# A message-passing kernel whose source columns come from copies and whose source rows come from gathers: 8 instead of 12 units of a round use column copies, and GpSimd gathers five more tiles

## The reference, cut to what matters

```
h_nodes = silu(x @ node_W1 + b) @ node_W2 + b                # 12500 x 64
h_edges = silu(edge_attr @ edge_W1 + b) @ edge_W2 + b        # 400000 x 64
msgs    = silu([h_nodes[dst], h_nodes[src], h_edges] @ msg_W1 + b) @ msg_W2 + b
agg     = segment_sum(msgs, dst) / max(counts, 1)
out     = layernorm(x + silu([x, agg] @ upd_W1 + b) @ upd_W2 + b) * ln_g + ln_b
result  = layernorm(x + out)
```

## Time and profile before

| | |
|---|---|
| median of 3 runs | 4963.27 us (4941.1 to 4977.42) |
| profiled execution: span from first to last instruction | 3612.0 us |
| profiled execution: its own time | not recorded for this kernel; the median is 1351.3 us above the span |
| TensorE (PE) busy | 2874.1 us, 80% |
| VectorE (DVE) busy | 2737.3 us, 76% |
| ScalarE (ACT) busy | 2994.3 us, 83% |
| GpSimd (POOL) busy | 2674.4 us, 74% |
| instructions in the trace | 103943 |
| DMA | 350.77 MB, mean 97 GB/s |

### The profile page before, as it was taken

How to read it: one execution, slowest core, us unless ns; L and a number is a source line. 1 busy time by engine, 2 the same in 40 slices (tenths; PEclk the granted TensorE clock), 3 DMA queues, 4 the chain that set the end, 5 groups by cost and what they waited for, 6 DMA issues and landing times.

```text
span 3612.0 us, 103943 instructions
## 1 busy us (share of the span) xinstructions
PE 2874.1 (80%) x16224; PEld 2219.4 (61%) x16224; DVE 2737.3 (76%) x20847; ACT 2994.3 (83%) x23073; POOL 2674.4 (74%) x2823
## 2 busy tenths in 40 slices
PE   4878888877878878888778888777778878877885
PEld 2666666666666666666666666656665656656664
DVE  4777778778777777777787777787777777877876
ACT  4998888888887888988888888888878888888785
POOL 4777777777777777777777777777777777777773
PEclk7687777677777777777777777777777776677766
DMA  7454444454444454444454444444444444444441
GB/s 225 78 113 100 87 94 100 89 102 96 95 95 86 96 102 90 101 100 88 93 103 85 102 96 95 99 95 87 98 92 99 101 89 96 90 92 102 96 95 43
DMA packets 263059, 350.77 MB, mean 97 GB/s; under 512 B 111714, under 2 KB 199121, under 8 KB 252514
## 3 DMA queue, kind: packets, MB, share of 16 engines
q1 hardware_dynamic: 169792, 246.77, 32.0%
q0 software_dynamic: 90624, 95.15, 14.5%
q10 hardware_dynamic: 1954, 2.14, 0.2%
HBM read 330.78 MB, written 13.01 MB: 95 GB/s over the span
## 4 chain that ended last, share of the span: by engine, by line
POOL 62%; issue 21%; PE 8%; DMA 4%; DVE 4%; DVEq 0%; ACT 0%; SPq 0%; ACTq 0%; POOLq 0%
POOL b_ring L834 62%; DMA b_ring<-b_table,src 4%; PE p_pre L696 2%; PE p_pre L702 1%; DVE colbuf L642 1%; PE p_sum L716 1%; PE p_hid L849 1%; DVE comb L939 1%; DMA work<-in_xT 1%; PE p_pre L705 0%; PE p_last L995 0%; PE p_last L996 0%; DVEq L627 0%; DVE stats L1032 0%; ACT colbuf L642 0%
## 5 line engine op out<-in xcount | busy, mean ns | idle before, releaser
L834 POOL DMA_INDIRECT b_ring<-b_table,src x2800 | 2652.0, 947 | 858.9 <-issue 844.8
L642 ACT COPY colbuf<-shared 64x4 uint8 x21134 | 2127.4, 190 | 159.9 <-issue 148.4
L642 DVE COPY colbuf<-shared 64x4 uint8 x17511 | 1377.6, 194 | 308.6 <-issue 301.9
L696 PE MATMUL p_pre<-wa_ring,comb 128*128 128x64 f32 x6250 | 1047.1, 329 | 0.0
L696 PEld LDWEIGHTS p_pre<-wa_ring,comb 128*128 128x128 f32 x6250 | 996.8, 245 | 0.9 <-issue 0.8
L727 ACT ACTIVATE comb<-p_hid,b_e 64x320 f32<-64x320 f32 x1250 | 652.8, 522 | 360.4 <-PE p_hid L849 350.9
L939 DVE SCALAR_TENSOR_TENSOR comb<-shared,p_const 64x640 f32<-64x640 int32 x625 | 554.0, 887 | 458.8 <-PE p_pre L696 336.2
L716 PEld LDWEIGHTS p_sum<-hot_ring,msg 128*65 128x65 f32 x6250 | 589.2, 181 | 500.0 <-DVE agg L949 265.0
L716 PE MATMUL p_sum<-hot_ring,msg 128*65 128x64 f32 x6250 | 649.5, 269 | 291.1 <-DVE agg L949 166.6
L702 PE MATMUL p_pre<-b_ring,ident 128*128 128x320 f32 (+1 forms) x1250 | 583.4, 559 | 341.4 <-DMA b_ring<-b_table,src 340.8
L849 PE MATMUL p_hid<-e_ring,w_e 128*128 128x320 f32 x1250 | 626.2, 591 | 49.0 <-DMA e_ring<-in_edgeT 40.0
(11 more groups left out here) (106 smaller groups left out, 599.2 us busy)
## 6 DMA issues: line engine op xcount, KB each, us to landing
e_ring<-in_edgeT SPq DMA_DIRECT2D x250, 320.0 KB
shared<-in_dst_row SPq DMA_DIRECT2D x125, 640.0 KB
b_ring<-b_table SPq DMA_DIRECT2D x3200, 0.2 KB
b_ring<-b_table,src POOLq DMA_INDIRECT x2800
e_ring<-in_edgeT SPq DMA_DIRECT2D x50, 400.0 KB
shared<-in_dst_row SPq DMA_DIRECT2D x25, 800.0 KB
wa_ring<-a_table SPq DMA_DIRECT2D x625, 16.0 KB
work<-in_xT SPq DMA_DIRECT2D x25, 250.0 KB
```

Of the source, the lines that this page charges most:

```text
L642: end = copy(colbuf[:, special % COLBUF, at:at + 1].bitcast(U8), of[j])
L696: return eng.matmul(p_pre[:, i % 2, k * H:(k + 1) * H], comb[:, i % COMBS, k * P:(k + 1) * P], wa_ring[:, i % RING, :], start=k == 0, stop ...
L834: eng.indirect_dma_start(b_ring[:, b_slot(i), k, :], None, b_table, bass.IndirectOffsetOnAxis(ap=src[:, u * TILES + k:u * TILES + k + 1], ...
```

## The change

The list of special units goes from 12 to 8, with smaller lists of columns. `ROW_TILE`, `load_rows`, `fetch_rows`, their semaphores and TensorE's wait for them are taken out, and GpSimd gathers the tiles: `by_pool(i)` becomes `gathered(i)`.

```
-SPECIAL = [1, 3, 5, 7, 9, 11, 13, 15, 17, 19, 21, 23]
+SPECIAL = [1, 4, 7, 10, 13, 16, 19, 22]
 COLS = dict(vector=58, scalar=70)
...
-LOAD = dict(vector=32, scalar=40)
-LISTED = 656
-ROW_TILE = (24, 3)
-ROWS_A_STEP = 8
-ROWS_FROM = 7
+LOAD = dict(vector=20, scalar=24)
+LISTED = 672
...
-    row_list_in = sem("row_list_in")
-    row_in = [sem(f"rows{q}_in") for q in range(4)]
...
     def gathered(i):
 
         return [k for k in range(TILES) if not (i in SPECIAL and k == TILES - 1)]
 
-    def by_pool(i):
-
-        return [k for k in gathered(i) if (i, k) != ROW_TILE]
...
-        load_rows(eng, 0)
-
-    def load_rows(eng, r):
...
-    def fetch_rows(eng, r, i):
...
-        for q, node in enumerate(nodes):
-            eng.dma_start(b_ring[first + q:first + q + 1, b_slot(unit), tile, :], b_table[ds(node, 1), :])\
-               .then_inc(row_in[q % len(row_in)], 16)
...
-        eng.wait_ge(row_list_in, 16 * ROUNDS + 16)
...
-            if 0 <= i - ROWS_FROM < P // ROWS_A_STEP:
-                fetch_rows(eng, r, i)
...
-            for k in by_pool(i):
+            for k in gathered(i):
                 eng.indirect_dma_start(b_ring[:, b_slot(i), k, :], None, b_table,
...
-            if j == ROW_TILE[0]:
-                for arrived in row_in:
-                    wait_alone(eng, arrived, (rr + 1) * (16 * P // len(row_in)))
```

More of the change, by code:

```diff
@@ L150, in program @@
         at += words
-    row_list = to_ab[0:1, :, :, :, :].rearrange("o s t q n -> o (s t q n)").bitcast(I32)[:, at:at + P]
-    assert at + P <= SR * 2 * 2 * GJ * H
+    assert at <= SR * 2 * 2 * GJ * H
     pad = sb("pad", [W, H], F32)
@@ L599, in gathered @@
         return [k for k in range(TILES) if not (i in SPECIAL and k == TILES - 1)]
-    def by_pool(i):
-        return [k for k in gathered(i) if (i, k) != ROW_TILE]
     def b_value(r, i):
-        each = [16 * len(by_pool(j)) for j in range(ROUND) if b_slot(j) == b_slot(i)]
-        so_far = [16 * len(by_pool(j)) for j in range(i + 1) if b_slot(j) == b_slot(i)]
+        each = [16 * len(gathered(j)) for j in range(ROUND) if b_slot(j) == b_slot(i)]
+        so_far = [16 * len(gathered(j)) for j in range(i + 1) if b_slot(j) == b_slot(i)]
         return sum(each) * r + sum(so_far)
@@ L745, in sync_first @@
         load_list(eng, LEADIN, LEADIN, HALF_AT, list_in[0])
-        load_rows(eng, 0)
-    def load_rows(eng, r):
-        eng.dma_start(row_list, a["rows"][ds(r * P, P)].unsqueeze(0)).then_inc(row_list_in, 16)
-    def fetch_rows(eng, r, i):
[L755 to L761, removed]
-        for q, node in enumerate(nodes):
-            eng.dma_start(b_ring[first + q:first + q + 1, b_slot(unit), tile, :], b_table[ds(node, 1), :])\
-               .then_inc(row_in[q % len(row_in)], 16)
-        if first + ROWS_A_STEP == P:
-            load_rows(eng, r + 1)
     def sync_last(eng):
-        eng.wait_ge(row_list_in, 16 * ROUNDS + 16)
         eng.wait_ge(list_in[0], 32 * ROUNDS + 32)
@@ L1091, in pool_general @@
         for u in range(EARLY):
-            eng.wait_ge(b_in[b_slot(u)], 16 * len(by_pool(u)))
+            eng.wait_ge(b_in[b_slot(u)], 16 * len(gathered(u)))
         with eng.Fori(0, UNITS) as u:
@@ L1208, in _laid_out @@
     d["dst_row"] = g["dst"].reshape(-1)
-    rows = g["src"].reshape(-1, ROUND, TILES, P)[:, ROW_TILE[0], ROW_TILE[1], :]
-    d["rows"] = np.concatenate([rows, np.zeros_like(rows[0:1])]).reshape(-1)
     special = g["src"].reshape(-1, ROUND, TILES, P)[:, SPECIAL, TILES - 1, :]
```

## The result

The changed kernel takes 4627.99 us, the median of four runs (4618.87 to 4634.18). The kernel before took 4960.24 us beside it, also of four (4941.1 to 4977.42). The ratio is 0.9333, 95% interval 0.9298 to 0.9368: 6.7% faster. I had forecast 3.2% slower and had given "faster by over 1%" one chance in ten.

What follows compares the result with a forecast made beforehand. GpSimd's gathers were taken to bound the kernel: a 3612.0 us span plus 156.5 us for 125 more gathers, with 1351.3 us around it held constant, gave 5120 us, 3.2% slower. The range was 5065 to 5200 us.

Steps and rivals of the forecast that it cites:

- 1351.3 us: Median time less profiled span, taken as time around the span and carried in the sum as a constant.
- What bounds the kernel: GpSimd's gathers bound it at 1.2519 us each, never held up by a full ring of source rows.
- Gathers: GpSimd's gathers go from 2800 to 2925, +125 at 1.2519 us each: +156.5 us, all on the bound.
- Pace of a gather: No change in GpSimd's pace as copies and single-row transfers go; at most 9 us either way.
- Column copies: 12,882 fewer copies, relieving ScalarE of 709 us and VectorE of 459 us, worth nothing while gathers bound.
- TensorE: Some 40 us less matmul work from fewer special tiles, off the path.
- SyncE: 3200 single-row DMAs go, relieving its queue of 1250 us; costed at nothing.
- B: Timed runs stretched evenly against the profile: a gather costs 1.720 us, 125 cost 215 us, 5178 us; chance 0.13.
- A: The forecast itself: gathers bound, the time around the span constant, 5120 us; chance 0.67.
- C: Time around the span shrinks with the program's instructions, by 292 us: 4828 us, faster; chance 0.10.
- D: Another engine or a transfer bounds the timed runs and hides the gathers: 4963 us, within 1%; chance 0.07.
- E: TensorE's clock falls to 1.2 GHz throughout with longer waits for gathers: 5426 us; chance 0.03.

Runs made afterwards that it cites:

- experiment 1: The kernel before, unchanged, profiled once more: 4977.24 us, with a span of 4974.7 us.
- experiment 15: The kernel after, with one of a unit's five sum matmuls done, four fifths of the sums left out: 4661.45 us, 0.9402 of the kernel before.
- experiments 2: The kernel before, still 12 special units, but without SyncE's single rows; GpSimd gathers that tile: 4688.55 us, 0.944 of the kernel before.
- 5: The kernel before with 8 special units; SyncE fetches 128 fixed rows, without node-number loads or register instructions: 4570.86 us, 0.9352 of the kernel before.
- 6: The kernel before, still 12 special units; SyncE fetches 128 fixed rows, without node-number loads or register instructions: 4641.0 us, 0.9356 of the kernel before.
- experiment 4: The kernel before with 8 special units; SyncE fetches 64 single rows instead of 128: 4557.64 us, 0.9328 of the kernel before.
- 8: The kernel before with 8 special units, single rows kept; ScalarE starts the edge feature and destination loads: 4987.71 us, 1.0072 of the kernel before.
- 9: The kernel after, with the edge feature and destination loads started by ScalarE instead of SyncE: 4877.25 us, 0.984 of the kernel before.
- 7: The kernel after, with 9600 unread semaphore increments on SyncE where the single rows stood: 4765.1 us, 0.9741 of the kernel before.
- 12: The kernel after, with 9600 semaphore increments on GpSimd ahead of the gathers in steps 7 to 22: 4767.39 us, 0.9637 of the kernel before.
- experiment 16: The kernel after, with each gather fetching 64 instead of 128 rows: 4608.57 us, 0.9301 of the kernel before.

## Why the prediction was wrong

**The step that failed first.** "I take the median as its time, so 1351.3 us is what lies around the span, and the sum carries it as a constant". No such time exists: in the repeated profile of the kernel before, span and time differ by 2.5 us (4974.7 and 4977.24), in the kernel after by 1.9. The trace was of an execution whose span is 26% shorter than the shortest timed one (4882.3 us). I had cited the Trainium skill (Runtime: NRT & Kernel Launch, The launch sequence), whose 9 to 15 us around a kernel say that 1351.3 us can't lie there, and set it aside as not explaining the gap. The traces agree that little lies around the span; the measured 1.9 and 2.5 us are below even that figure. That page of the Trainium skill spoke against the step, not only beside it.

**What bounds the kernel.** "So GpSimd is never held up by a full ring of source rows" holds for the execution that the earlier trace rows come from, and not for the timed ones, where it is held up for 1520 us (experiment 1).

**Gathers.** The count is right, x2925. But the +156.5 us, "all on the bound", is wrong: in the timed runs GpSimd has waits to put them into. 200 more of them together with 25,800 fewer copies (12 to 4 special units) leave the time within 1%; alone they were not tried.

**Pace of a gather.** Right: 953 ns median and about 1.25 us from one to the next when nothing is waited for (745.8 us of "issue" in 2433 gaps is 0.307 us each). The Trainium skill (SBUF — State Buffer, Who interferes with whom) has a VectorE copy in a two-port mode lock GpSimd out. No run here shows whether these copies run in such a mode. No lock shows in the gathers' durations, as in the earlier trace rows: one lasts 946 ns beside 17,511 copies, 952 beside 11,674, 948 beside none.

**Column copies.** "Worth nothing" was nearly right for the kernel after (1.1%, together with 100 more gathers, hardly told from none) and wrong by sign where the rows stay (+6.0%). No rival had such an interaction.

**TensorE.** That 40 us less of its work count for nothing fits: without four fifths of its sum matmuls the kernel was no faster, though at a lower clock (experiment 15).

**SyncE.** "TensorE's waits are for b_ring, not these, in the rows shown, so I cost the relief at nothing." This is the term that carries the result: the change gains 6.7%, and taking out the rows alone gains 5.6% of 4951.68 us, **277 us**, 263 in medians (4951.68 - 4688.55). I had the right queue and the right things behind it. The 1250 us for what it was relieved of were too low: with the 400 loads of node numbers, which I left out, the rows took 1680 us of SyncE in the execution shown and 2746 us in the repeated one, counted in the traces. And I didn't ask what happens if SyncE runs late. Its cover was a lead of edge features over TensorE: TensorE waited 40.0 us for them in the execution shown and 312.6 us in the repeated one.

**The rivals.** B was wrong with A: the gather's own pace isn't stretched, GpSimd waits. C was the only one on the right side, and for a reason that doesn't exist; that 4828 us lies nearer to 4628 than the rest is luck. D named the right thing, "something else bounds the timed runs", and priced it at no change, with a chance of 0.07. Once something else is the bound, the work that the change takes from *that* decides, and the chain of the repeated execution leads through SyncE, from which the change takes those 2746 us. E is out: the clock rose to 0.657 from 0.608 and the time fell.

**What would show it.** The counts held, and nearly the 947 ns of a gather (952). The sign that the bound had moved was put down right: "A GpSimd that waits for pre_mm for more than a few us". So was the weak place: "The prediction fails most simply if the surrounding time is not constant". I had called that the simplest way to fail and given the forecast 0.67 against it.

**What the runs show, and how far.** Shown: the gain comes with the removal of what SyncE executes to find the rows' addresses (experiments 2, 5, 6); the DMAs alone cost nothing; the price needs more than half of the rows (4). Well supported: the price is that edge features come late, since TensorE's wait for them goes and comes with it (16.6, 312.6 and 932.1 us) and most of it is gone when they don't queue behind the rows (8 against 9, with the reservation made there). Other instructions in that place bring 4.1 of the 6.7 points back with the same wait (7), but 3.0 points come back on GpSimd without it (12), so 7 alone doesn't part the queue from the number of instructions. Argued only: that the stalls of 0.7 us are what makes SyncE late. The traces have 1015 of over 600 ns in the rows' groups where the quick execution has none, with the same medians, but no run took the stalls away.

**What stays open.** Why one execution ran without them. Why fewer column copies make SyncE's rows later (1.0599), when the copies are on other engines. And what sets the 7.2 us a unit of the kernel after: not the gathers' packets; fewer copies with more gathers, and fewer sums of TensorE at a lower clock, gained nothing. Extra instructions on SyncE and GpSimd hurt; ScalarE and VectorE were not tried in this way. No version tried beats the kernel after by more than the intervals; experiment 4 (0.9328) leaves rows out, and experiment 16 (0.9301) half of the gathers.

## What to carry to other kernels

Before arguing from a trace, set its span against the time. A gap that nothing known fills can mean, as here, that the trace is of an unlike execution, and then no engine's slack in it can be trusted: take the queues that the change relieves and ask for each what would follow if it ran late in the timed runs. A queue that issues many small things ahead of a few large ones can cost nothing while its lead lasts and much once it is used up; here half of the small things were free and all of them cost 6 to 14%. That price came with the instructions that find an address, not with the transfers alone.

## What the hardware did that I had not expected

- The same program ran in 3612.0 us once and in 4882 to 4976 us (spans) in the 41 runs beside the experiments, with the granted clock at 0.748 and at 0.600 to 0.616, and the median durations of SyncE's instructions unchanged.
- Instructions for which the trace shows no wait start 0.71 to 0.73 us apart, mostly on VectorE and ScalarE at the same instants, for some 3 us in the stretch shown (1008.46 to 1011.34 above), and SyncE's shortest instructions, of 29 and 37 ns, last up to 1.41 us, about twice that step. No instruction packets moved in the stretch shown.
- An instruction with a median of 17 ns, on an engine that waits 961 us in all, cost 94 ns of the kernel's time when there were 2500 of them, 63 ns when there were 5000, and 16 ns when 9600 stood in two thirds of the units.
- 3200 DMAs of one 256-byte row from fixed addresses, 244 ns of SyncE each, cost nothing measurable (0.9352 [0.9331, 0.9374] with them, 0.9333 [0.9298, 0.9368] without).
